# Convolution stage of a four-layer image kernel: products with D on ScalarE, a second outer tap on VectorE, four u tiles, the pixel split on GpSimd

## What is computed

```python
xz = x @ Win
xb, z = jnp.split(xz, 2, axis=-1)                   # 256 channels each
xb = conv_general_dilated(xb, conv_w, (1, 1), ((1, 1), (1, 1)), ..., feature_group_count=256)   # 3 x 3, one filter per channel
xb = silu(xb + conv_b)                              # u, in row order and turned for the column scans
x_dbl = einsum('bcl,cd->bdl', xs_flat, Wxproj)      # dt, B and C
y = selective_scan(u, delta, A, B, C, ...) + u * Dv
z = silu(z)
```

## Time and profile before

| what | value |
|---|---|
| runs | 4011.5, 4012.12 (median), 4024.51 us |
| the profiled execution | 4020.02 us, span of the trace 4017.8 us |
| convolution stage, first tap of round 0 to first tap of round 31 | 2916.02 to 3292.14 us of the span, 376.12 us |
| busy over the whole span | PE 93%, DVE 80%, ACT 68%, POOL 36% |

### The profile page before, as it was taken

The page is one execution under the profiler, slowest core; times in us unless marked ns, Lnnn a source line. Parts: engine busy times, 40 slices in busy tenths (PEclk is TensorE's granted clock), DMA queues, the critical chain, the costliest instruction groups (busy, mean ns, idle before and its releaser), DMA issues. The chain is left out here.

```text
span 4017.8 us, 73101 instructions
## 1 busy us (share of the span) xinstructions
PE 3724.5 (93%) x24794; PEld 2958.8 (74%) x24794; DVE 3200.9 (80%) x7763; ACT 2751.1 (68%) x6205; POOL 1447.4 (36%) x1716
## 2 busy tenths in 40 slices
PE   7999996999999999999999999998799976888898
PEld 5777774899888998889998898885577752333347
DVE  6899995777787777877778777777777878998885
ACT  5788884677776777767777666675855547777753
POOL 6788882000010000110001100004325667888873
PEclk8999997999999999999999999999899985877789
DMA  8877761000010000110001000003234446656567
GB/s 214 202 200 204 194 174 33 18 20 25 17 41 25 23 22 17 38 30 23 24 17 35 25 14 10 10 9 111 99 107 163 151 167 186 189 177 216 168 191 226
DMA packets 291316, 383.07 MB, mean 95 GB/s; under 512 B 43520, under 2 KB 162048, under 8 KB 290176
## 3 DMA queue, kind: packets, MB, share of 16 engines
q1 hardware_dynamic: 260176, 310.73, 25.7%
q0 software_dynamic: 29184, 67.27, 6.4%
q10 hardware_dynamic: 1584, 0.40, 0.1%
HBM read 205.59 MB, written 119.54 MB: 81 GB/s over the span
## 5 line engine op out<-in xcount | busy, mean ns | idle before, releaser
L959 ACT ACTIVATE l_ph<-l_T 128x512 fp32r<-128x512 f32 x1024 | 612.4, 598 | 549.7 <-PE l_T L864 549.7
L1076 DVE TENSOR_TENSOR l_pl<-l_T,l_ph 128x512 fp32r<-128x512 f32 x1024 | 707.7, 691 | 274.8 <-ACT l_ph L959 274.0
L1065 DVE CUSTOM_DVE_ANT_0 l_pr<-l_S,l_zero 128x512 f32<-128x512 f32 x1024 | 705.3, 689 | 75.8 <-PE l_S L787 13.3
L964 ACT ACTIVATE l_pr<-l_pr,l_st 128x512 f32<-128x512 f32 x1024 | 731.5, 714 | 1.1 <-DVE l_st L1071 1.0
L876 PE MATMUL l_O<-l_ph,l_vh 128*128 128x256 f32 x2048 | 662.0, 323 | 12.6 <-DVE l_pl L1076 12.4
L1108 POOL TENSOR_TENSOR l_xs<-l_xs,l_bob 128x128 f32<-128x128 f32 x128 | 57.2, 461 | 1646.5 <-DMA l_xs<-x 1645.3
L864 PE MATMUL l_T<-l_ident,l_pr 128*128 128x128 f32 x4096 | 613.3, 272 | 0.0
L864 PEld LDWEIGHTS l_T<-l_ident,l_pr 128*128 128x128 f32 x4096 | 508.0, 140 | 136.4 <-issue 0.2
L877 PE MATMUL l_O<-l_ph,l_vl 128*128 128x256 f32 x2048 | 578.1, 282 | 0.0
L878 PE MATMUL l_O<-l_pl,l_vh 128*128 128x256 f32 x2048 | 577.0, 282 | 0.0
L785 PE MATMUL l_S<-l_kh,l_qh 128*128 128x512 f32 x1024 | 418.1, 408 | 1.4 <-DVE l_st L1065 1.2
(11 more groups left out here) (268 smaller groups left out, 8151.7 us busy)
## 6 DMA issues: line engine op xcount, KB each, us to landing
l3b_u<-ub SPq DMA_DIRECT2D x256, 256.0 KB, 3.0
l_kq<-l_hl SPq DMA_DIRECT2D x192, 128.0 KB, 5.5
l_kq<-l_hl POOLq DMA_DIRECT2D x192, 128.0 KB, 4.3
zs<-l_tmp SPq DMA_DIRECT2D x64, 256.0 KB, 3.7
ub<-l3a_u SPq DMA_DIRECT2D x32, 512.0 KB, 3.3
l3b_z<-zs SPq DMA_DIRECT2D x64, 256.0 KB, 3.7
yz<-l3b_z SPq DMA_DIRECT2D x64, 256.0 KB, 3.3
l3b_dt<-yz SPq DMA_DIRECT2D x32, 512.0 KB, 4.5
```

What stands on the lines that cost most here:

```text
L959: e.activation(ph[:, i, :], psT[:, i, :], ACT.Copy).then_inc(p_hi, 1)
L964: e.activation(pr[:, s, es], pr[:, s, es], ACT.Exp, bias=st[:, s, 9:10], scale=SC, accum_out=st[:, s, 10 + k:11 + k]).then_inc(exped, 1)
L1065: e.tensor_tensor_reduce(pr[:, s, ks], psS[:, bk, :], zero[:].broadcast_to([128, 512]), 1.0, -3.0e38, ALU.add, ALU.max, st[:, s, kc:kc + 1 ...
L1076: e.tensor_tensor(pl[:, i, :], psT[:, i, :], f32(ph[:, i, :]), ALU.subtract).then_inc(p_lo, 1)
```

## The change

The tap (0, 0) leaves TensorE, which keeps four outer taps (24 products for the two halves in place of 30), and is a fifth operation in VectorE's taps, with both inputs in SBUF. ScalarE multiplies u by D, right behind the two Silus of u; the scale on VectorE waits for that product and no longer for GpSimd. GpSimd keeps the sum into acc and the turned copy, and takes over the low parts xl of the next image's pixels (the first image's remain on VectorE). There are four u tiles in place of three, and two dv tiles. On SyncE the four stores of dm are issued behind the store of u and the planes, no longer ahead of them and of the stores of sk. The weights of one tap less are prepared in the layer before, by one DMA less and slightly shorter GpSimd operations.

```diff
@@ convolve
-        U = P.sb("u", [128, 2, 3, 512])
-        dv = P.sb("dv", [128, 512])
+        U = P.sb("u", [128, 2, 4, 512])
+        dv = P.sb("dv", [128, 2, 512])
...
@@ sync
-                if 0 < g <= N:
-                    bb, c0 = divmod(g - 1, 8)
-                    w.wait_ge(d_done, g)
-                    for q in range(4):
-                        e.dma_start(f32(D[32 * bb:32 * bb + 28, 512 * c0 + 128 * q:512 * c0 + 128 * q + 128]), f32(dm[32 * q:32 * q + 28, (g - 1) % 2, :])).then_inc(d_out[(g - 1) % 2], 16)
                 if g > N - 8 and g <= N:
...
                     if g >= 3 and (g - 3) % 8 == 7:
                         store_turned((g - 3) // 8)
+                if 0 < g <= N:
+                    bb, c0 = divmod(g - 1, 8)
+                    w.wait_ge(d_done, g)
+                    for q in range(4):
+                        e.dma_start(f32(D[32 * bb:32 * bb + 28, 512 * c0 + 128 * q:512 * c0 + 128 * q + 128]), f32(dm[32 * q:32 * q + 28, (g - 1) % 2, :])).then_inc(d_out[(g - 1) % 2], 16)
@@ tensor
-                for j, (dr, dc) in enumerate(((0, 0), (0, 2), (2, 0), (2, 1), (2, 2))):
+                for j, (dr, dc) in enumerate(((0, 2), (2, 0), (2, 1), (2, 2))):
@@ scalar
                         e.activation(u, u, ACT.Silu, bias=cb[:, h:h + 1]).then_inc(activated, 1)
+                    b, ch = divmod(g - 1, 8)
+                    for h in range(2):
+                        w.wait_ge(activated, 2 * (g - 1) + h + 1)
+                        if g - 1 >= 9:
+                            w.wait_ge(skipped, 2 * (g - 10) + h + 1)
+                        e.activation(dv[:, h, :] if b else part(acc[:, h, :], 0, ch), u_of(g - 1, h), ACT.Copy, scale=cD[:, 2 * b + h:2 * b + h + 1]).then_inc(skip_v, 1)
@@ vector
-                if g >= 3:
-                    w.wait_ge(u_out[g % 3], 16 * (g // 3))
-                    w.wait_ge(turned_u, 2 * (g - 3) + h + 1)
+                if g >= 4:
+                    w.wait_ge(u_out[g % 4], 16 * (g // 4))
+                    w.wait_ge(turned_u, 2 * (g - 4) + h + 1)
...
-                e.scalar_tensor_tensor(u, X[:, 0:8, 1:65], ct[:, h, 3:4], u, ALU.mult, ALU.add).then_inc(tapped, 1)
+                e.scalar_tensor_tensor(u, X[:, 0:8, 0:64], ct[:, h, 3:4], u, ALU.mult, ALU.add).then_inc(tapped, 1)
+                w.wait_ge(tapped, 8 * g + 4 * h + 3)
+                e.scalar_tensor_tensor(u, X[:, 0:8, 1:65], ct[:, h, 4:5], u, ALU.mult, ALU.add).then_inc(tapped, 1)
...
-                    w.wait_ge(skipped, 2 * g + h + 1)
+                    w.wait_ge(skip_v, 2 * g + h + 1)
                     e.tensor_tensor(u, psB[:], u, ALU.mult).then_inc(times_B, 1)
...
-                    for m in loads(g):
-                        load(m)
@@ gpsimd
+            def load(m):
+                r = slice(8 * (m % 8) + 1, 8 * (m % 8) + 9)
+                w.wait_ge(padded, 8 - AHEAD)
+                w.wait_ge(padded_hi, m + 1 - AHEAD)
+                e.tensor_tensor(xl[:, r, 1:65], xr[:, m % 2, :].rearrange("p (r c) -> p r c", c=64), f32(xh[:, r, 1:65]), ALU.subtract).then_inc(padded, 1)
+
+            def skip(g):
                 b, ch = divmod(g, 8)
                 for h in range(2):
                     o = part(acc[:, h, :], b, ch)
-                    w.wait_ge(activated, 2 * g + h + 1)
-                    if b == 0:
-                        e.tensor_scalar(o, u_of(g, h), cD[:, h:h + 1], None, ALU.mult).then_inc(skipped, 1)
-                    else:
...
+                    w.wait_ge(skip_v, 2 * g + h + 1)
+                    e.tensor_tensor(o, o, turned(dv[:, h, :], b), ALU.add).then_inc(skipped, 1)
...
+            for g in range(N + 1):
+                if g - 1 >= 8:
+                    skip(g - 1)
+                if g < N:
+                    for m in loads(g):
+                        load(m)
```

More of the change, by code:

```diff
@@ L1175, in spread_tap @@
                 return io["taps"][k:k + 1].rearrange("(a t) c -> a t c", a=1).broadcast_to([128, 1, 256])
-            for dst, src in ((win, io["L3_conv_Win"]), (V.tmp[:, 0:1, :], spread_tap(0)), (V.tmp[:, 1:2, :], spread_tap(2)),
-                             (V.tmp[:, 2:5, :], io["taps"][6:9].rearrange("(a t) c -> a t c", a=1).broadcast_to([128, 3, 256])),
+            for dst, src in ((win, io["L3_conv_Win"]), (V.tmp[:, 0:1, :], spread_tap(2)),
+                             (V.tmp[:, 1:4, :], io["taps"][6:9].rearrange("(a t) c -> a t c", a=1).broadcast_to([128, 3, 256])),
                              (V.ct[:, 0, 0:3], io["taps"][3:6, 0:128].rearrange("t p -> p t")), (V.ct[:, 1, 0:3], io["taps"][3:6, 128:256].rearrange("t p -> p t")),
-                             (V.ct[:, 0, 3:4], io["taps"][1:2, 0:128].rearrange("t p -> p t")), (V.ct[:, 1, 3:4], io["taps"][1:2, 128:256].rearrange("t p -> p t")),
+                             (V.ct[:, 0, 3:5], io["taps"][0:2, 0:128].rearrange("t p -> p t")), (V.ct[:, 1, 3:5], io["taps"][0:2, 128:256].rearrange("t p -> p t")),
                              (V.wx[:], io["wx32"].rearrange("(h p) d -> p h d", p=128)), (V.cb[:], io["L3_conv_conv_b"].rearrange("(h p) -> p h", p=128)),
@@ L1384, in gpsimd @@
                     e.memset(f32(K.D[:]), 1.0).then_inc(cleared, 1)
-                    w.wait_ge(conv_weights, 272)
+                    w.wait_ge(conv_weights, 256)
                 if g == 10:
@@ L1451, in __init__ @@
         self.tmp = tile("tmp", [128, 6, 256])
-        self.th, self.tl = tile("th", [128, 5, 256], F32R), tile("tl", [128, 5, 256], F32R)
+        self.th, self.tl = tile("th", [128, 4, 256], F32R), tile("tl", [128, 4, 256], F32R)
         self.wh, self.wl = tile("wh", [128, 512], F32R), tile("wl", [128, 512], F32R)
         self.xb = tile("xb", [128, 4, 9, 66])
-        self.ct = tile("ct", [128, 2, 4])
+        self.ct = tile("ct", [128, 2, 5])
         self.xh, self.xl = tile("xh", [128, 66, 66], F32R), tile("xl", [128, 66, 66], F32R)
@@ L1485, in u_of @@
         def u_of(g, h):
-            return U[:, h, g % 3, :]
+            return U[:, h, g % 4, :]
         ps = P.ps("c", [128, 5, 512])
         psD = P.ps("d", [128, 2, 512])
-        x_in, d_out, z_out, u_out = P.slots("x_in", 2), P.slots("d_out", 2), P.slots("z_out", 3), P.slots("u_out", 3)
+        x_in, d_out, z_out, u_out = P.slots("x_in", 2), P.slots("d_out", 2), P.slots("z_out", 3), P.slots("u_out", 4)
         skip_out = P.slots("skip_out", 2)
@@ L1497, in convolve @@
         free = P.slots("free", 5)
-        padded_hi, activated, turned_u, topped = (P.sem(n) for n in ("padded_hi", "activated", "turned_u", "topped"))
+        padded_hi, activated, turned_u, topped, skip_v = (P.sem(n) for n in ("padded_hi", "activated", "turned_u", "topped", "skip_v"))
         padded, tapped, parts, d_done, times_B = (P.sem(n) for n in ("padded", "tapped", "parts", "d_done", "times_B"))
-        skip_v, skipped, skip_t = P.sem("skip_v"), P.sem("skipped"), P.sem("skip_t")
+        skipped, skip_t = P.sem("skipped"), P.sem("skip_t")
         use = {}
@@ L1563, in sync @@
                 w.wait_ge(z_out[s], 16 * len(range(s, 2 * N, 3)))
-                w.wait_ge(u_out[s], 16 * len(range(s, N, 3)))
+            for s in range(4):
+                w.wait_ge(u_out[s], 16 * len(range(s, N, 4)))
             for s in range(2):
@@ L1649, in scalar @@
                         if g >= 2:
-                            w.wait_ge(tapped, 6 * (g - 2) + 3 * h + 3)
+                            w.wait_ge(tapped, 8 * (g - 2) + 4 * h + 4)
                         e.activation(xb[:, (2 * g + h) % 4, 1:9, 1:65], ps[:, i, :].rearrange("p (r c) -> p r c", c=64), ACT.Copy).then_inc(free[i], 1)
@@ L1668, in scalar @@
                         if g:
-                            w.wait_ge(tapped, 6 * (g - 1) + 3 * h + 3)
+                            w.wait_ge(tapped, 8 * (g - 1) + 4 * h + 4)
                         above = xb[:, (2 * g + h) % 4, 8, 1:65] if g % 8 < 7 else f32(xh[:, 0, 1:65])
@@ L1742, in vector @@
                     taps(g, 1)
-                    for m in loads(g):
-                        load(m)
         def gpsimd(e):
             w = Waits(e)
-            for g in range(N):
+            def load(m):
[4 more added lines that the diff above has]
+            def skip(g):
                 b, ch = divmod(g, 8)
@@ L1751, in gpsimd @@
                     o = part(acc[:, h, :], b, ch)
-                    w.wait_ge(activated, 2 * g + h + 1)
-                    if b == 0:
-                        e.tensor_scalar(o, u_of(g, h), cD[:, h:h + 1], None, ALU.mult).then_inc(skipped, 1)
-                    else:
[L1756 to L1759, removed]
+                    w.wait_ge(skip_v, 2 * g + h + 1)
+                    e.tensor_tensor(o, o, turned(dv[:, h, :], b), ALU.add).then_inc(skipped, 1)
                     if b == NI - 1:
-                        w.wait_ge(skipped, 2 * g + h + 1)
+                        w.wait_ge(skipped, 2 * (g - 8) + h + 1)
                         if ch:
```

14 lines of the change are left out of this document (7 added, 7 removed).

## The result

Nine runs of the changed kernel have a median of 4004.91 us (3991.98 to 4008.84), nine of the kernel before 4013.51 (4005.76 to 4024.51). The ratio of the means, 4001.5 and 4016.3 us, is 0.9963, 95% interval 0.9947 to 0.998: 15 us faster, between 8 and 21. The medians are only 8.6 us apart. The forecast was 4010 us with no difference that can be told; the time lies in the range, 5 us under the forecast. By the means the gain is just outside the 12 us that I had called the same, by the medians inside it.

The account below looks back on a forecast made before the run. TensorE bounds images 0 to 2 before; afterwards VectorE, at 9.42 us a round plus stops by GpSimd, bounds images 1 to 3. Rounds -7.8 and end +5.6 give -2: 4018 profiled, 4010 us on the median's scale, range 3984 to 4037.

Parts of the forecast that it names:

- VectorE's 9.42 us a round: VectorE's own work without disturbance: five taps in two halves 7.62, small 0.59, scale 1.2, against TensorE's 9.8 us a round.
- the forecast of 368.3: First tap of round 0 to that of round 31: images 80.0, 95.1, 101.5 and 91.7 us, against 376.12 before.
- rival 3: TensorE's clock falls in its new gaps, products take about twice 0.238 us; +15 us, 4025 us, chance 0.05.
- The boundary of image 1: Late pixels at an image boundary: planes issued about 6 us earlier, 0.7 us left of the 5, bounds 0 and 5.
- three such places: Image boundaries where pixels load late behind 4 MB of planes; the image with ScalarE's 11.00 us wait has 5.2 us extra.
- The end: After the last first tap: last taps +1.8 us, last store of u +3.8; together +5.6 us, bounds 0 and 8.
- The sum: Stage total: rounds -7.8 us, with the end -2; profiled 4018 us, 4010 on the median's scale.
- Rival 1: GpSimd operations stopping VectorE's taps (holds) fall luckily, 0.6 us each: -27 us, 3985 us, chance 0.27.
- the forecast's prices: VectorE's loss per GpSimd operation stopping taps: first sum 0.59 or 0.97 us, second 0.90 or 1.28, split 0.90, copy 0.67.
- The signs for rivals 1 and 2: VectorE's taps would show a mean near 0.85 us for rival 1, above 1.4 for rival 2.
- rival 2: Each GpSimd operation stopping VectorE's taps costs its whole length: 408 us for the rounds, +38 us, 4050 us, chance 0.19.
- four tiles, and a store of u that no longer stands behind dm: VectorE's wait for free u tiles goes; with the store clear of 3.16 us of dm issues, a round of slack.

## Why the prediction came out as it did

- **The own work and the bound.** VectorE's 9.42 us a round and the passing of the bound to it were right: 11.76 us a round in image 1 (11.8), 12.6 in image 2 (12.6), 13.1 in image 3 (13.0), 79.8 us for image 0 (80.0). In images 2 and 3 the mean hides two errors that offset each other, see below. Most of what the 31 rounds gained on the forecast of 368.3 lies in image 1: 91.0 in place of 95.1.
- **Each image's first round, the first error.** I charged eight rounds of image 1 with sums. The sums of round 8 run beside round 9, so round 8 takes 9.79 us; that is 2 us. The same slip is in the other images: rounds 16 and 24, which still have the sums of the image before, take 10.95 and 11.27 us, 1.7 under the 12.6 and 13.0 of the forecast. There slow rounds make up for it (round 23 with 13.97 us, where two splits hold taps; round 26 with 14.88, see rival 3), so that images 2 and 3 came out close by luck. The boundary of image 1, for which I had left 0.7 us, gave 0.8: in round 11 the pixels came 1.36 us late, and the split with them, so it ran beside `small` and line 1710, where it holds nothing, and the round took 10.94 us (rows of the changed kernel, GpSimd and VectorE in order of time):

```profile
3020.06 1.20 POOL L1760 TENSOR_TENSOR l_xl<-ahead,l_xh 128x512 fp32r<-128x512 f32 x1 [2.01 <-ACT l_xh L1641]
```

```profile
3020.68 0.74 DVE L1710 SCALAR_TENSOR_TENSOR l3a_u<-l_xb,l_ct,l3a_c 128x512 f32<-128x512 f32 x1
3021.46 0.75 DVE L1712 SCALAR_TENSOR_TENSOR l3a_u<-l_xb,l_ct,l3a_u 128x512 f32<-128x512 f32 x1
```

  These two and the rounding of the forecast's steady rounds leave under 1 us of the 4.1. The third of the "three such places" was read wrongly: image 3 has no next image whose pixels could be late, and before the change ScalarE waits there 5.75 us for a store of z instead.
- **The end.** +5.6 us forecast, +3.9 found. The mechanism stands: the last store of u goes 3287.51 - 3276.52 = 11.0 us behind the last Silu of u (forecast 11.4, 7.6 before), as these rows of the changed kernel's end show:

```profile
3276.52 0.72 ACT L1664 ACTIVATE l3a_u<-l3a_u,l_cb 128x512 f32<-128x512 f32 x1 [3.67 <-DVE l3a_u L1720]
...
3283.83 0.43 SPq L1552 DMA_DIRECT2D ub<-l3a_u  x1
3284.31 3.16 SPq L1559 DMA_DIRECT2D l_D<-l3a_dm  x4
3287.51 0.53 SPq L1552 DMA_DIRECT2D ub<-l3a_u  x1
3292.16 0.81 SPq L1901 DMA_DIRECT2D l3b_u<-ub  x2
```

  The last taps ended 11.4 us behind the last first tap, not 11.9, and the next stage followed the last store sooner, by 4.7 us against 5.5.
- **The sum.** -2 us forecast for the stage with its end, -9.0 measured: -12.9 for the rounds and +3.9 for the end. With 12 us as the limit of what can be told, "the same" was the right class for the stage by itself; the runs give 15 us with an interval that takes in the stage's 9.
- **Rival 1** (lucky holds). Not in the changed kernel: 67 us over in 256 taps, with 88 holds, is 0.76 a hold, not 0.6, and the steady rounds have the forecast's prices. But it is real: in the kernel with the split back one sum costs 0.04.
- **The signs for rivals 1 and 2** were mis-sized. By the prices in the prediction the 256 taps have a mean of 0.93 us under rival 1 and 1.21 under rival 2, not 0.85 and 1.4; my forecast makes it 1.04, and 1.01 was measured. Rival 2's sum leaves out its last term, too: it is 411 us, which makes 4053.
- **Rival 2** (full length). No hold in the round shown costs more than 0.91 us, and the shortest sum is 1.28.
- **Rival 3** (clock). In small it came true: the granted clock falls to a mean of 0.91 in image 3. While VectorE is in round 26, TensorE idles 2.08 us ahead of `spread`, waiting for VectorE's dm; from 3207.24 us on its 12 products of `outer` come 0.43 us apart in place of 0.238, at a granted clock of 0.50 (the lower of its two levels, 1.2 GHz), and VectorE waits for them:

```profile
3212.87 0.75 DVE L1710 SCALAR_TENSOR_TENSOR l3a_u<-l_xb,l_ct,l3a_c 128x512 f32<-128x512 f32 x1 [1.60 <-PE l3a_c L1575]
```

  At 0.238 they would have ended some 2 us sooner and this wait would be gone. It is the 1.6 us by which round 26 is longer than a steady one; VectorE's other waits for TensorE in image 3 are 0.4 to 0.6 us each. The other rounds there are VectorE's.
- **What I had not taken apart.** The prediction gave "four tiles, and a store of u that no longer stands behind dm" one effect. The runs part them: the place of the dm stores is worth 24 us in the kernel before and 10 in the changed one, the tile nothing, the moved tap costs 13, the moved split 10 (the last two undone in the changed kernel, one at a time; where TensorE is the bound, as with the tap back, the split costs nothing, so they do not add up). From the kernel with the dm stores alone moved, 352.2 us, the rest of the change goes up to 363.2: by these traces it is faster only because its one good part is worth more than the others cost.

## What to carry to other kernels

Before work is moved to an engine with idle time, ask what its instructions do to the engine beside it: here an operation of 0.60 us on VectorE became 0.82 us of waiting for VectorE when GpSimd did it, and giving it back saved all of the 0.82, since by its place it keeps a sum from holding a tap. When a change has several parts, price each alone, and expect that the prices do not add up; a block of four small DMAs moved in one queue was worth more than the whole. And where one stage has rounds with different neighbours, a split of the work between engines can be chosen per round.

## What the runs showed of the hardware that I had not expected

A GpSimd multiplication of one tile by a column, 1.56 us alone, runs beside VectorE's two-input taps at a cost of 0.06 to 0.41 us (in image 2, where it reads its tile turned, it takes 2.1 us itself), whereas a sum, a split or a plain copy of the same size stops them until it ends: replacing 48 sums by products took 41 us from the stage with GpSimd busy as before.
